# Graph network, four layers on 16 graphs: keys and queries as rows of 128, another order, and idle matmuls

## The reference

```python
# layer 0: attention with 8 heads, one number per node and head as query, one as key
feat_proj = (feats @ fc_w + fc_b).reshape(bs, n, HEADS, dim).transpose(0, 2, 1, 3)
q = feat_proj @ q_w + q_b
k = feat_proj @ k_w + k_b
logits = q + jnp.swapaxes(k, -1, -2)
masked = logits + (1.0 - adj_mat[:, None]) * NEG
masked = jax.nn.leaky_relu(masked, negative_slope=0.01)
attn = jax.nn.softmax(masked, axis=-1)
out = attn @ feat_proj
out = out.transpose(0, 2, 1, 3).reshape(bs, n, HEADS * dim)
out = out @ fp_w + fp_b + feats
return jax.nn.sigmoid(out)
```

## Time and profile before

| | |
|---|---|
| median of 3 runs | 2171.48 us (2170.83 to 2172.71) |
| the profiled execution, its own time | 2170.93 us |
| its span, first to last instruction | 2168.9 us |
| granted TensorE clock, mean | 0.995 |
| PE matmul busy | 2080.0 us (96%), 12818 instructions |
| DVE busy | 1608.3 us (74%) |
| ACT busy | 1517.9 us (70%) |
| POOL busy | 777.2 us (36%) |

### The profile page before, as it was taken

How to read it: one execution, slowest core, us unless ns; L and a number is a source line. 1 busy time by engine, 2 the same in 40 slices (tenths; PEclk the granted TensorE clock), 3 DMA queues, 4 the chain that set the end, 5 groups by cost and what they waited for, 6 DMA issues and landing times. The chain is left out here.

```text
span 2168.9 us, 36700 instructions
## 1 busy us (share of the span) xinstructions
PE 2080.0 (96%) x12818; PEld 1763.5 (81%) x12818; DVE 1608.3 (74%) x4782; ACT 1517.9 (70%) x2968; POOL 777.2 (36%) x888
## 2 busy tenths in 40 slices
PE   7899999999999999999999999999999999999987
PEld 6778797887978878797887978878797887979865
DVE  5687887868778687886868778686877868788643
ACT  6678594966849677694967859587694967859532
POOL 2334334343423424334343424433333343433311
PEclk9999999999999999999999999999999999999999
DMA  3101001010100101001010100101001010100100
GB/s 121 49 21 45 25 1 44 26 45 25 43 27 2 44 25 45 25 1 46 24 45 25 45 25 2 44 25 45 25 6 53 12 44 25 45 6 1 47 3 5
DMA packets 47320, 65.74 MB, mean 30 GB/s; under 512 B 3744, under 2 KB 21536, under 8 KB 47008
## 3 DMA queue, kind: packets, MB, share of 16 engines
q1 hardware_dynamic: 47136, 63.41, 9.1%
HBM read 59.21 MB, written 4.19 MB: 29 GB/s over the span
## 5 line engine op out<-in xcount | busy, mean ns | idle before, releaser
L648 PE MATMUL banks<-F,PT 128*128 128x128 f32 x4096 | 543.3, 276 | 2.3 <-DVE PT L1241 1.6
L648 PEld LDWEIGHTS banks<-F,PT 128*128 128x128 f32 x4096 | 507.0, 192 | 15.1 <-DVE PT L1241 2.1
L478 POOL TENSOR_TENSOR HS<-HT,HS 128x512 fp32r<-128x512 f32 x64 | 83.6, 1307 | 535.5 <-ACT HS L1008 535.5
L1241 DVE COPY PT<-banks 128x512 f32<-128x512 f32 x256 | 175.6, 686 | 116.0 <-PE banks L642 115.3
L944 ACT ACTIVATE PT<-banks 128x512 f32<-128x512 f32 x256 | 151.2, 591 | 89.0 <-PE banks L642 86.7
L979 ACT ACTIVATE F<-banks,dcols 128x512 f32<-128x512 f32 x288 | 193.6, 684 | 25.7 <-PE banks L512 21.5
L445 POOL TENSOR_SCALAR tiles<-tiles,rden 128x512 f32<-128x512 f32 x192 | 143.7, 762 | 97.0 <-DVE rden L1231 96.8
L415 POOL TENSOR_TENSOR rstd<-var,mhalf 128x4 f32<-128x4 f32 x64 | 72.4, 1130 | 268.6 <-DVE var L1144 268.6
L508 PE MATMUL banks<-HS,WH 128*128 128x512 f32 (+1 forms) x368 | 155.8, 423 | 1.7 <-ACT HS L907 1.4
L445 POOL TENSOR_SCALAR U<-U,rden 128x512 f32<-128x512 f32 x192 | 130.6, 700 | 72.9 <-DVE rden L1231 72.8
L509 PE MATMUL banks<-HS,WLO 128*128 128x512 f32 (+1 forms) x368 | 145.8, 396 | 0.0
(11 more groups left out here) (218 smaller groups left out, 5346.6 us busy)
## 6 DMA issues: line engine op xcount, KB each, us to landing
adjN<-in_adj_dram SPq DMA_DIRECT2D x32, 1024.0 KB, 5.6
adjT<-in_adjt_dram SPq DMA_DIRECT2D x16, 1024.0 KB, 5.6
xin<-in_x_dram SPq DMA_DIRECT2D x18, 256.0 KB, 2.9
out_dram<-X SPq DMA_DIRECT2D x16, 256.0 KB, 5.9
F<-in_wraw_dram SPq DMA_DIRECT2D x1, 1076.0 KB, 9.2
adjT<-in_c2w_dram SPq DMA_DIRECT2D x1, 1024.0 KB, 11.4
PT<-in_fcw_dram SPq DMA_DIRECT2D x1, 512.0 KB, 5.1
PT<-in_fpw_dram SPq DMA_DIRECT2D x1, 512.0 KB, 6.1
```

Source lines behind the costliest of these rows:

```text
L478: pool.tensor_tensor(HL[s], HT[s][:, :], HH[s].bitcast(F32), ALU.subtract).then_inc(S["h_new_low"], 1)
L648: last = pe.matmul(B[s][:, 3, part(j)], PT[s][:, k, part(j)], G[s][:, k, h * DIM:(h + 1) * DIM], start=(h == 0 and j == 0 and k == 0), sto ...
L1241: dve.tensor_copy(PT[s][:, j, :], pt_bank(s, j)).then_inc(S["pt_dve"], 1)
```

## The change

1. Keys and queries become rows. One product of three float32r matmuls of 512 columns (`kq`), with `VQH`/`VQL` of 128 columns as the stationary side, gives for every node the rows 0 to 7 and 32 to 39 (minus the keys) and 64 to 71 and 96 to 103 (the queries). ACT takes it with a scale that is 1 on rows 32 to 39 and 96 to 103 and 0 elsewhere (`KS`, rounded to float32r), DVE subtracts (`KR`): the first rows hold the rounded value, the others what it lacks.
2. A head's keys are spread by one float32r matmul of 512 columns: `pick`, a 0/1 column per head broadcast to 128, times `KR`, in place of four float32 transposes.
3. The queries are picked out of `KR` by four matmuls of 8 columns, in the strand `keys`; the third value product now waits for `kq_rows`, and no value product waits for `qk`.
4. The five idle matmuls ahead of the queries go (graphs 2 to 15); 16 come ahead of the second value product (graphs 1 to 15). In the last graph 24 idle matmuls become 26.
5. `den` and `rden` get one copy per entry of the ring of three; waits that others imply are dropped; `cand_a` waits for `r` alone in layer 2.
6. The start vector of the sum (`acc_start`) is made before `h_low` of the graph, not after the value copies; `ob` is computed in the setup ahead of `M`.
7. All entries of `TURN` and `START` are new.

```diff
+            KR.append(sb(f"KR{s}", [P, NODES], F32R))
...
-                if g >= SLOTS:
-                    for k in range(5):
-                        pe.matmul(B[s][:, 3, :], WH[:, 0:P], WH[:, 0:4 * P])
-                pe.wait_ge(*own("h_low", g, 0))
...
-                for t in range(TILES):
-                    last = mm3(B[s][:, 3, 16 * t:16 * t + 16], (HH[s][:, part(t)], HL[s][:, part(t)]),
-                               (VQH[:, :], VQL[:, :]))
-                last.then_inc(S["qk_banked"], 1)
+                pe.wait_ge(*own("h_high", g, 0))
+                high(B[s][:, 3, :], (VQH[:, :], VQL[:, :]), (HH[s], HL[s]))
+                pe.wait_ge(*own("h_low", g, 0))
+                low(B[s][:, 3, :], (VQH[:, :], VQL[:, :]), (HH[s], HL[s])).then_inc(S["kq_banked"], 1)
...
+                    if i == 1 and g >= 1:
+                        busy(B[s][:, 0, :], 16)
...
-                        pe.wait_ge(*after("qk", g))
+                        pe.wait_ge(*after("kq_rows", g))
...
+                yield
+                pe.wait_ge(*after("kq_rows", g))
+                for t in range(TILES):
+                    last = pe.matmul(B[s][:, 0, HEADS * t:HEADS * (t + 1)], KR[s][:, part(t)], pick[:, HEADS:2 * HEADS])
+                last.then_inc(S["qk_banked"], 1)
...
-                    for t in range(TILES):
-                        last = pe.transpose(B[s][:, 0, part(t)],
-                                            QK[s][:, t, HEADS + h:HEADS + h + 1].broadcast_to([P, P]), ident[:, :])
-                    last.then_inc(S["kb_banked"], 1)
+                    pe.matmul(B[s][:, 0, :], pick[:, h:h + 1].broadcast_to([P, P]),
+                              KR[s][:, :]).then_inc(S["kb_banked"], 1)
...
-                    busy(B[s][:, 1, :], 24)
+                    busy(B[s][:, 1, :], 26)
...
+                act.wait_ge(*after("kq_banked", g))
+                act.activation(KS[s], B[s][:, 3, :], ACT.Identity, bias=0.0, scale=cols[:, CI["qlow"]:CI["qlow"] + 1])\
+                    .then_inc(S["kq_high"], 1)
...
+                dve.wait_ge(*after("kq_high", g))
+                dve.tensor_tensor(KR[s][:, :], B[s][:, 3, :], KS[s].bitcast(F32), ALU.subtract).then_inc(S["kq_rows"], 1)
...
-START = (0.000, 130.369, 260.718, 391.050, 521.380, 651.749, 782.086, 912.423, 1042.760,
+START = (0.000, 132.248, 264.495, 396.735, 528.996, 661.212, 793.461, 925.711, 1057.960,
```

More of the change, by code:

```diff
@@ L234, in build @@
         HT = [sb(f"HT{s}", [P, NODES]) for s in SL]
-        hN = [sb(f"hN{s}", [P, NODES]) for s in SL]
+        hN, KR = [], []
+        for s in SL:
+            with nc.sbuf_tensor(f"hN{s}", [P, NODES], F32) as t:
+                hN.append(t)
+            KR.append(sb(f"KR{s}", [P, NODES], F32R))
         X = [sb(f"X{s}", [P, TILES, DIM]) for s in SL]
@@ L245, in build @@
         smin = [sb(f"smin{s}", [P, TILES]) for s in SL]
-        den = [sb(f"den{s}", [P, TILES]) for s in SL]
+        den = [sb(f"den{s}", [P, RING, TILES]) for s in SL]
         gate = [sb(f"gate{s}", [P, 4, TILES]) for s in SL]
-        rden = [sb(f"rden{s}", [P, TILES]) for s in SL]
+        rden = [sb(f"rden{s}", [P, RING, TILES]) for s in SL]
         B = [ctx.enter_context(nc.psum_tensor(f"banks{s}", [P, 4, 512], F32)) for s in SL]
@@ L322, in build @@
         HH = [HS[s][:, 0, :] for s in SL]
+        KS = [U[s][:, TILES - 1, :].bitcast(F32R) for s in SL]
         HL = [HS[s][:, 1, :] for s in SL]
@@ L531, in weights @@
                     pe.matmul(B[1][:, 2, 2 * h:2 * h + 2], fcT[:, part(h)], cols[:, CI["qw"]:CI["qw"] + 2])
-                pe.matmul(B[1][:, 3, 0:HEADS], dcol("qkw").broadcast_to([P, P]), cols[:, 0:HEADS]).then_inc(vq_banked, 1)
+                pe.matmul(B[1][:, 3, 0:HEADS], dcol("qkw").broadcast_to([P, P]), cols[:, 0:HEADS])
+                for h in range(HEADS):
+                    pe.matmul(B[1][:, 3, P:2 * P], cols[:, h:h + 1].broadcast_to([P, P]), fp[:, part(h)], start=(h == 0), stop=False)
+                pe.matmul(B[1][:, 3, P:2 * P], col("fpb").broadcast_to([P, P]), ident[:, :], start=False, stop=True)\
+                    .then_inc(vq_banked, 1)
                 yield
@@ L536, in weights @@
                 last.then_inc(m_banked, 1)
-                yield
-                pe.wait_ge(vq_ready, 1)
-                for h in range(HEADS):
-                    pe.matmul(B[1][:, 3, 0:DIM], cols[:, h:h + 1].broadcast_to([P, P]), fp[:, part(h)], start=(h == 0), stop=False)
-                pe.matmul(B[1][:, 3, 0:DIM], col("fpb").broadcast_to([P, P]), ident[:, :], start=False, stop=True)\
-                    .then_inc(m_banked, 1)
                 yield
@@ L748, in layer2 @@
                     pe.wait_ge(*after("rows_high", turn))
-                    pe.wait_ge(*after("adjacency", g))
+                    if layer == 0:
+                        pe.wait_ge(*after("adjacency", g))
                     for t in range(TILES):
@@ L793, in layer3 @@
                 pe.wait_ge(*own("h_high", g, 3))
-                pe.wait_ge(*own("residual", g, 2))
                 high(B[s][:, 1, :], W("c1"), (HH[s], HL[s]))
@@ L928, in softmax @@
                         yield
-                        if h >= 1:
-                            act.wait_ge(*after("rden", turn - 1, t + 1))
                         act.wait_ge(*after("logits", turn, t + 1))
@@ L1228, in denominators @@
                         dve.wait_ge(*after("exped", g * HEADS + h, t + 1))
-                        if h >= 1:
-                            dve.wait_ge(*after("attn", g * HEADS + h - 1, t + 1))
-                        dve.reciprocal(rden[s][:, t:t + 1], den[s][:, t:t + 1]).then_inc(S["rden"], 1)
+                        dve.reciprocal(rden[s][:, h % RING, t:t + 1], den[s][:, h % RING, t:t + 1]).then_inc(S["rden"], 1)
             def tile_copies(g):
@@ L1257, in scaled_rows @@
                     dve.wait_ge(*after("s_exped", g, t + 1))
-                    dve.reciprocal(rden[s][:, t:t + 1], den[s][:, t:t + 1]).then_inc(S["rden1"], 1)
+                    dve.reciprocal(rden[s][:, 0, t:t + 1], den[s][:, 0, t:t + 1]).then_inc(S["rden1"], 1)
                     dve.wait_ge(*after("rden1", g, t + 1))
@@ L1345, in cand_a @@
                 s = g % SLOTS
-                dve.wait_ge(*after("hn", cell))
-                dve.wait_ge(*after("r", cell))
+                dve.wait_ge(*after("r" if cell % (LAYERS2 + 1) < LAYERS2 else "hn", cell))
                 dve.scalar_tensor_tensor(F[s][:, 3, :], F[s][:, 0, :], 1.0, F[s][:, 2, :], ALU.add, ALU.mult)\
@@ L1490, in rows @@
         return _np.array(values, _np.float32)
-    none = rows(0, 0, 0, 0, 0)
+    none, heads_one = rows(0, 0, 0, 0, 0), _np.ones(HEADS, _np.float32)
     moving, still = rows(1, 1, 1, 0, 1), rows(2, 2, 2, 1, 0)
     moving_one, still_one = rows(0, 0, 0, -1, 0), rows(0, 0, 0, 0, -1)
-    nq = _np.zeros((P, AUG), _np.float32)
+    nq, pick = _np.zeros((P, AUG), _np.float32), _np.kron(_np.eye(2, dtype=_np.float32), _np.tile(_np.eye(32, HEADS, dtype=_np.float32), (2, 1)))
     for b in range(BLOCKS):
```

121 lines of the change are left out of this document (60 added, 61 removed), and 103 rows, old and new, of the table TURN.

## The result

The changed kernel takes 2162.43 us (median of 8 runs, 2156.58 to 2165.75), the kernel before, run beside it, 2171.68 us (median of 8, 2169.57 to 2172.71): ratio 0.9954, 95% interval 0.9944 to 0.9964, 9.2 us less. Forecast were 20.4 us less, 2151.1. The eight runs of the changed kernel lie wider apart than those of before, and go with the mean granted clock of TensorE: 2156.58 and 2157.05 at 0.994, 2158.51 at 0.992, 2162.41, 2162.45 and 2163.72 at 0.990, 2164.90 and 2165.75 at 0.987. The profiled execution is the fastest of them, 2156.58 us (span 2154.8), 14.35 less than the one profiled before; so its trace has to explain 14.35. The median lies 5.9 above it; that this is the clock is read from the runs' clocks alone, since only one execution has a trace.

The account below looks back on a forecast made before the run. PE was taken as the bound outside the window, DVE's and POOL's chain inside it. Keys -18.2, window -2.8 and setup +0.6 summed to -20.4 us, giving 2151.1 us against the median; range 2138 to 2166.

Parts of the forecast that it names:

- the side that had 0.85: The whole kernel measured faster, below 2167.1 us: chance 0.85.
- the likeliest case: The whole kernel at the forecast 2151 us, its own range 2144 to 2158: chance 62%.
- The keys: PE's heads: one matmul replaces four transposes, 0.20 us less for six heads, 1.2 per graph, -18.2 us in 15 graphs.
- Rival 1: PE's heads: keys no cheaper, since four transposes and one long matmul both stream 512 columns; 2169 us, 4%.
- The window: From accY to layer 2's begin: gate 1.2 us earlier, layer 2 begins sooner, -0.2 per graph, -2.8 us in all.
- The clock: PE in the steady windows: granted clock stays 1.00, as the longest idle time left is under 1.60 us.
- Rival 4: PE's clock falls in each window, idle matmuls and products behind take twice as long, 4 us per graph: 2207 us, 2%.
- The idle matmuls: Ahead of the second value product: cost 0, covered by the residual sum moved behind the statistics.
- The order: Layer 2's second pass, products with R split: 5.3 us of cover is enough for the GRU cell, 0 taken.
- Setup and the first window: Before the steady graphs: ob ahead of M puts the first keys +0.6 us later; idle matmuls in the first window cost 0.
- Rival 2: POOL, ACT or DVE is late with tiles through the heads, 0.7 us per graph: 2161.5 us, 16%.

Follow-up runs that it names:

- experiment 9: The kernel of experiment 4 with a head's keys spread by four matmuls of 128 columns instead of one of 512: 2164.63 us, ratio 0.9963.
- experiment 8: The kernel of experiment 4 with DVE's adjacency step AN behind hN and QN instead of between KR and hN: 2146.48 us, ratio 0.9882.
- experiment 1: The changed kernel with 23 idle matmuls ahead of the second value product instead of 16: 2152.97 us, ratio 0.9916.
- experiment 2: The changed kernel with none of the 16 idle matmuls ahead of the second value product: 2184.51 us, ratio 1.0061.
- experiment 3: The changed kernel with a head's keys spread by four matmuls of 128 columns instead of one of 512: 2172.93 us, ratio 1.0002.
- experiment 4: The changed kernel with DVE's residual sum (L1169) back ahead of the gate: 2143.77 us, ratio 0.9874.
- experiment 5: The changed kernel with POOL's addition (L467) waiting for the end of DVE's gate dot products: 2165.80 us, one run.

## Why the prediction was wrong

The kernel is faster by 9.2 us, where 20.4 were forecast; 2162.43 lies in the range (to 2166) and on the side that had 0.85, but the likeliest case did not come. By its own steps:

**The keys** were right, and a little large in size: -1.09 us per graph by experiment 9, some 16 in place of 18.2. That experiment has four float32r matmuls and not the four float32 transposes of before, so it is a near measure of the term, not the term itself. L622 takes 0.23 behind a product of 512 columns and 0.31 to 0.32 behind four transposes of 128. As the step said, six heads count: the second head's saving became a wait (L730 waits 0.32 for `HT` behind the first turn, 0.18 before), and by experiment 9 the one in the window is worth nothing either. Rival 1 is out: four float32r matmuls of 128 columns take 0.39 to 0.48 where one of 512 takes 0.23 to 0.32. The rule of columns plus 2.5 ns for an isolated matmul, which the Trainium skill states, TensorE: Matmul & The Clock Gate, section Back-to-back issue gap, would, as an estimate, give both some 0.22; in these streams it does not hold.

**The window** is the step that failed, in the sentences "The gate starts 1.2 earlier, `var` is ready at 1155.5" and "`hN` starts at about 1158.0 instead of 1158.37". The gate did start earlier, into POOL's addition, and was held by it. Before, DVE's work at that place (L1175 and L1156) read one operand from PSUM and ran beside POOL's L469 unhindered, and the gate began just when POOL had ended. I added up DVE's durations as if they did not depend on what POOL does, and read the 1.43 of POOL's power as its own, where it is 1.02 without `AN` beside it (experiment 8). Measured: -0.34 for `var` instead of the -1.2; then KR, the residual sum and AN take 2.4 us where 1.7 passed before between `var` and `hN`, as reckoned. The term is +0.48 per graph, +6.7 us in place of -2.8, and the wait for the residual sum 1.63 in place of 0.7.

**The clock** was the second failure. The argument was that the idle time left would be under the 1.60 us that kept the clock before. It became 1.63, and at about that length the clock fell in some windows and not in others. Nor was 1.60 the longest wait that kept the clock before: one window of that kernel has 1.89, and its clock stays too. So a length of wait alone was no ground for the argument. Rival 4 named it, at 2% and 4 us per graph for every window; it costs 1.3 us in some. In the profiled execution that is 4 us beside the long window's part. The median has 5.9 more, which goes with the runs' clocks and is not traced. Experiments 1 and 2 show both sides of it.

**The idle matmuls** cost nothing, as said, but my reason ("their cover is the residual sum") was half of it: without them the kernel is 22 us slower.

**The order**: the second pass of layer 2 has no wait of PE, so 0 was right there. Not foreseen: one window of 14 has DVE's sum in another place, by 0.014 us between two due times (734.102 against 601.872 + 132.216 = 734.088); 3.7 us. And from the second turn of layer 2 to the next `accY` PE's stream is 1.5 us shorter per graph, 1.1 of it keys by experiment 9; the other 0.4, which helped the forecast, no run here separates.

**Setup and the first window**: the first keys came at 25.70 instead of 22.96, 1.0 of that a later transfer, against +0.6 forecast. Yet the heads of graph 0 end 1.1 us earlier (ACT's tanh at 91.34 instead of 92.43): from the first keys to there 65.6 us pass instead of 69.5. Keys by four matmuls take back 0.5 to 0.6 of that (66.3 in experiment 3, 66.1 in 9), so the keys are a small part of it, and what the rest is no run separates. Then the clock, 0.82 from there to the first layer 2 before, stays at 1.00:

```profile
95.00:124.00 29.00, 21.50 (x102) 16.37 (x100) 21.43 (x80) 8.70 (x18) 8.68 (x7) 0.82 0.09 27
```

```profile
95.00:121.00 26.00, 21.17 (x106) 15.49 (x106) 21.38 (x77) 8.78 (x19) 8.24 (x7) 1.00 0.06 18
```

(The first is the kernel before, the second the changed one.) I had given that window 0; all up to there came to -3.0 us. Part of this is luck of the profiled execution: in eight of the eleven kernels of the experiments the clock does fall in this stretch, and their first layer 2 begins at 121.0 to 123.6, not at 120.5.

Rival 2's time, 2161.5, is nearly the result, but not its mechanism: the only steady wait of PE outside the window is the 0.32 for `HT`. The forecasts that held: the period of 128.2 (128.5), no wait for QK, `hN` within 0.5 us. Those of a wait of 0.7 at L730 for `HT` and of a clock of 1.00 in all steady windows did not. That the median lies in the range is luck in part: the begin and the end gave what a window lost.

## What to carry to other kernels

Before adding up a chain on DVE, lay POOL's timeline beside it and ask of each overlap where both read their operands. An instruction that is moved to an earlier place may arrive in a neighbour's shadow; work with an operand in PSUM fits there, as the sum did in experiment 4. A wait of PE that ends last can be worth filling with idle matmuls even when nothing gets shorter by it (here 9.5 us for the last seven), and where an order comes from due times, every graph's order is to be compared, not one.

## What was not expected of the hardware

- DVE and POOL hold each other up, either way. A dot product of 0.28 us took 1.37 beside POOL's addition, and a subtraction of 0.69 took 1.80. The other way, POOL's power of 4 columns took 1.02 us beside KR (one operand in PSUM) and 1.43 or 1.69 beside AN, ending with it, although AN reads one tile of SBUF and not two.
- The clock of PE falls after one wait of 1.63 to 1.68 us and not after another just like it: in 3 of 13 such windows of the changed kernel, in 9 of the 13 of experiment 5, often in neighbouring ones. It fell with waits of 0.46 in experiment 9 too, and did not fall behind the waits of 1.59 to 1.89 in all 14 windows of the kernel before, nor behind the one of 2.38 in experiment 1. What beside the length of the wait decides is left open.
- A float32r matmul of 512 columns takes 0.23 us to the next start behind another of 512 columns, and more behind short ones: 0.31 to 0.33 behind float32 transposes of 128 columns, about 0.29 behind float32r matmuls of 128 (experiments 3 and 9), 0.31 behind float32r ones of 16 (the kernel before, 1153.77). So it is not the change of type alone; how much is type and how much width is not separated.
